# A pre-norm transformer layer with a mixture of experts on one core: routing work and weight loads placed inside the attention's turns, in one program block

## The reference

```python
x = x + attention(layernorm(x))     # 32 query heads, 8 key/value heads of 64, rotary, causal softmax
x = x + experts(layernorm(x))

gate_logits = einsum('bsd,de->bse', x, gate_kernel)          # 8 experts
top_k_weights, top_k_indices = top_k(gate_logits, 2)
top_k_weights = softmax(top_k_weights)
h0 = x @ w0[e]; h1 = x @ w1[e]                                # 256 -> 512
out = sum over the 2 chosen e of weight * (silu(h0) * h1) @ wo[e]   # 512 -> 256
```

## Time and profile before

| | us |
|---|---|
| median of 3 runs | 856.08 (851.24 to 856.58) |
| profiled execution | 854.13 |
| its span, first to last instruction | 852.2 |
| last matmul of attention ends | 556.6 |
| first expert matmul starts | 635.3 |

### The profile page before, as it was taken

How to read it: one execution, slowest core, us unless ns; L and a number is a source line. 1 busy time by engine, 2 the same in 40 slices (tenths; PEclk the granted TensorE clock), 3 DMA queues, 4 the chain that set the end, 5 groups by cost and what they waited for, 6 DMA issues and landing times. The chain is left out here.

```text
span 852.2 us, 18997 instructions
## 1 busy us (share of the span) xinstructions
PE 753.5 (88%) x5895; PEld 637.9 (75%) x5895; DVE 493.2 (58%) x1943; ACT 481.4 (56%) x1537; POOL 460.3 (54%) x690
## 2 busy tenths in 40 slices
PE   3699999999999999999999999826039999999994
PEld 2578888888888888888888888622027888888883
DVE  5797666666666667667567667384942333333331
ACT  1568777777777777777777777625212222222221
POOL 1456656556566565565565666346633545444452
PEclk9899999999999999999999999968559999999998
DMA  5434122122121221221221212058631223333230
GB/s 191 133 112 106 36 60 65 37 63 62 40 64 51 50 63 46 56 60 42 63 54 48 63 40 63 14 169 253 202 137 26 47 45 53 52 54 52 45 50 2
DMA packets 51905, 61.16 MB, mean 72 GB/s; under 512 B 10368, under 2 KB 45440, under 8 KB 51552
## 3 DMA queue, kind: packets, MB, share of 16 engines
q1 hardware_dynamic: 40144, 48.48, 20.0%
q0 software_dynamic: 7488, 9.36, 6.8%
q10 hardware_dynamic: 4176, 2.11, 0.9%
HBM read 26.34 MB, written 9.32 MB: 42 GB/s over the span
## 5 line engine op out<-in xcount | busy, mean ns | idle before, releaser
L818 POOL TENSOR_SCALAR probs<-exps,inv_sums 128x128 f32<-128x128 f32 x256 | 97.0, 379 | 195.7 <-DVE inv_sums L676 135.3
L557 ACT COPY pT<-probsT 128x384 f32<-128x384 f32 x256 | 122.0, 477 | 80.4 <-PE probsT L434 80.4
L434 PE MATMUL probsT<-tables,probs 128*128 128x128 f32 x768 | 129.8, 278 | 5.4 <-ACT pT L557 4.0
L550 ACT ACTIVATE exps<-masked,neg_max 128x256 f32<-128x256 f32 x256 | 127.5, 498 | 0.0
L819 POOL TENSOR_SCALAR probs<-exps,inv_sums 128x256 f32<-128x256 f32 x256 | 124.4, 486 | 0.0
L548 ACT ACTIVATE exps<-masked,neg_max 128x128 f32<-128x128 f32 x256 | 103.2, 403 | 37.0 <-DVE neg_max L670 36.8
L1411 POOL DMA_INDIRECT out<-y,to_token x39 | 61.9, 1587 | 102.4 <-DVE y L1380 78.2
L421 PE MATMUL scores<-kT,qT 64*128 64x128 f32 (+1 forms) x1024 | 103.3, 342 | 5.1 <-DMA qT<-rotated 5.1
L670 DVE CUSTOM_DVE_ANT_0 masked<-scores,tables 128x256 f32<-128x256 f32 x256 | 107.5, 420 | 0.0
L668 DVE CUSTOM_DVE_ANT_0 masked<-scores,tables 128x128 f32<-128x128 f32 x256 | 72.1, 282 | 54.2 <-PE scores L421 32.4
L434 PEld LDWEIGHTS probsT<-tables,probs 128*128 128x128 f32 x768 | 87.2, 141 | 19.5 <-issue 9.7
(11 more groups left out here) (156 smaller groups left out, 1876.4 us busy)
## 6 DMA issues: line engine op xcount, KB each, us to landing
qT<-rotated SPq DMA_DIRECT2D x256, 64.0 KB, 2.2
kT<-k_cos SPq DMA_DIRECT2D x64, 128.0 KB, 3.4
experts_w_out<-w_in SPq DMA_DIRECT2D x16, 512.0 KB, 4.6
raw<-w_attn SPq DMA_DIRECT2D x20, 256.0 KB, 3.3
experts_w_out<-w_out SPq DMA_DIRECT2D x2, 2048.0 KB, 9.7
out<-x_all SPq DMA_DIRECT2D x8, 256.0 KB, 2.3
xn_rows<-experts_w_out ACTq DMA_DIRECT2D x4, 512.0 KB, 4.5
x_all<-x SPq DMA_DIRECT2D x1, 1792.0 KB, 10.6
```

Source lines behind the costliest of these rows:

```text
L434: mm = nc.tensor.transpose(p_bank[:, at:at + P], probs[:, h, at:at + P], ident)
L550: nc.scalar.activation(exps[:, h, P:3 * P], masked[:, h, P:3 * P], ACT.Exp, bias=neg_max[:, h, 1:2], scale=-1.0, accum_out=sums[:, h, 1:2] ...
L557: nc.scalar.copy(pT[:, n % 2, h, :], p_bank[:, 0:3 * P]).then_inc(pT_done, 1)
L818: nc.gpsimd.tensor_scalar(probs[:, h, 0:P], exps[:, h, 0:P], inv_sums[:, h, 0:1], 1.0, ALU.mult, ALU.mult)
```

## The change

The three program blocks become one, and each function returns the lists of its engines, which are called one after the other: attention's, routing's tail, the experts'. SBUF is laid out so that the expert weights of expert e, 16 KB per partition (`experts_w`, slot e: part 0 is hi, part 1 is where the raw half lands and is later overwritten with lo), lie over attention buffers that are free at a known point: slots 0 and 1 over the q weights, 2 over k and v, 3 and 4 over the output weights, 5 over kT, qT and v_all, 6 over pT and oT, 7 over probs, exps and tables. `w_out` of expert e lies over xT, k_cos, by_cos, rotated, xn, masked and the first rows of x_all.

In the turns of batches 1 to 7 the second layer norm of the batch before is computed two tiles at a time, stored to DRAM and taken to logits. PE gets three new steps at a turn's end: "t" (g = 5, four transposes), "l" (g = 7, four matmuls) and, in turn (7, 3), "r", the ranks of the first 12 tiles (batches 0 to 5). The last batch chooses experts for these 12 tiles, makes their lane codes, and loads and splits the first expert slots. POOL no longer subtracts; DVE makes all low parts. Newton takes three steps of three operations. The identity has its own small DMA at the start. After attention, `tail_*` does the rest: the last batch's layer norm, its logits, choice and ranks, rows, codes and tokens, and slots 3, 7, 5, 4 and 6. The first expert matmul waits for all 16 half slots (`slot_split`).

The core of the diff:

```diff
+FIRST_BATCHES = 6
+FIRST_TILES = FIRST_BATCHES * TT
...
     def projects(b, g):
...
+        if g in (5, 7) and b > 0:
+            return {5: "t", 7: "l"}[g], b - 1, 0
+        if (b, g) == (LAST, 3):
+            return "r", 0, 0
...
@@ sync, turn(b, g) @@
+            if g == 5 and b > 0:
+                rt["store_rows"](sp, b - 1)
...
+            if b == LAST:
+                preload(g)
...
+        def preload(g):
+
+            if g == 1:
+                rt["load_w_out"](sp, 7)
+            if g == 2:
+                sp.wait_ge(q_ps, LAST * KV_HEADS + 4)
+                rt["load_slot"](sp, 0, 0)
+            if g == 3:
+                rt["load_slot"](sp, 0, 1)
...
+                rt["load_slot"](sp, 2, 0)
+            if g == 4:
+                rt["load_slot"](sp, 2, 1)
...
+                rt["load_w_out"](sp, 2)
+            if g == 5:
+                sp.wait_ge(q_ps, TURNS)
+                rt["load_slot"](sp, 1, 0)
+                rt["load_slot"](sp, 1, 1)
+                rt["load_w_out"](sp, 0)
+                rt["load_w_out"](sp, 1)
+            if g == 6:
...
+                rt["load_w_out"](sp, 4)
+            if g == 7:
+                sp.wait_ge(s_ps, (TURNS - 1) * GROUP)
+                rt["load_slot"](sp, 3, 0)
+                rt["load_slot"](sp, 3, 1)
...
+        sp.wait_ge(exp_done, TURNS * GROUP)
+        rt["load_w_out"](sp, 5)
+        rt["load_w_out"](sp, 6)
+        sp.wait_ge(pT_ps, TURNS * GROUP)
+        rt["load_slot"](sp, 7, 0)
+        rt["load_slot"](sp, 7, 1)
+        sp.wait_ge(o_ps, TURNS)
+        rt["load_slot"](sp, 5, 0)
+        rt["load_slot"](sp, 5, 1)
+        sp.wait_ge(y_ps, BATCH)
+        for slot in (4, 6):
+            rt["load_slot"](sp, slot, 0)
+            rt["load_slot"](sp, slot, 1)
...
@@ tensor, turn(b, g) @@
-            whole = projects(b, g)[0] is not None
+            whole = projects(b, g)[0] in ("x", "k", "v")
...
@@ scalar, turn(b, g) @@
+                if what == "t":
+                    rt["copy_rows"](act, of)
...
+            if (b, g) == (LAST, 3):
+                rt["gap_exp"](act, 0)
+            if b == LAST and g in (4, 5):
+                rt["slot_hi"](act, {4: 0, 5: 2}[g], 0)
             exponentials(b, g, 2)
+            if b == LAST and g in (4, 5):
+                rt["slot_hi"](act, {4: 0, 5: 2}[g], 1)
+            if (b, g) == (LAST, 6):
+                rt["store_weights"](act, 0)
+            if (b, g) == (LAST, 7):
+                rt["slot_hi"](act, 1, 0)
             exponentials(b, g, 3)
+            if (b, g) == (LAST, 7):
+                rt["slot_hi"](act, 1, 1)
             copy_probs(b, g, 0)
...
@@ vector, turn(b, g) @@
+            if g == 2 and b > 0:
+                rt["row_stats"](dve, b - 1)
             split_in_slot(b, g, 2)
             inverses(b, g, 2)
+            if g == 3 and b > 0:
+                rt["row_moments"](dve, b - 1)
+                rt["row_newton"](dve, 0, 1)
+            if g == 4 and b > 0:
+                rt["row_newton"](dve, 1, 3)
+                rt["row_normalise"](dve, b - 1)
...
+            if b == LAST:
+                routing(g)
...
+        def routing(g):
+
+            if g == 0:
+                rt["choose"](dve, 0, 0)
+            if g == 1:
+                rt["choose"](dve, 0, 1)
+                rt["both"](dve, 0)
+            if g == 5:
+                rt["choice_weights"](dve, 0)
+                rt["first_lanes"](dve)
+            if g == 6:
+                rt["lane_codes"](dve, 0)
+                rt["slot_lo"](dve, 0, 0)
+                rt["slot_lo"](dve, 0, 1)
+            if g == 7:
+                rt["slot_lo"](dve, 2, 0)
+                rt["slot_lo"](dve, 2, 1)
...
         out_lo(LAST, KV_HEADS - 2)
         inverses(LAST, KV_HEADS - 1, 3)
+        rt["read_logits"](dve, LAST - 1)
+        for half in range(2):
+            rt["slot_lo"](dve, 1, half)
         out_lo(LAST, KV_HEADS - 1)
...
+    def tail_tensor(pe):
+        transposes(pe, LAST)
+        gate_logits(pe, LAST)
+        ranks(pe, r["rank_bank"], 1)
         pe.wait_ge(block_lane_done, 1)
...
+    def tail_scalar(act):
+        act.wait_ge(y_added, BATCH)
+        nc.scalar.dma_start(t["out"][LAST].rearrange("(t p) e -> p t e", p=P),
+                            r["x_all"][:, LAST * TT:TILES, :]).then_inc(out_started, 16)
+        for half in range(2):
+            slot_hi(act, 3, half)
+        act.wait_ge(xn_done, BATCH)
+        nc.scalar.dma_start(rows_dram(LAST), xn).then_inc(xn_out, 16)
+        copy_rows(act, LAST)
+        for half in range(2):
+            slot_hi(act, 7, half)
+        gap_exp(act, 1)
+        store_weights(act, 1)
+        for half in range(2):
+            slot_hi(act, 5, half)
         act.wait_ge(block_hot_done, 1)
         nc.scalar.activation(block_codes[:, :, 1, :], block_codes[:, :, 1, :], ACT.Copy,
                              scale=lane).then_inc(block_lane_done, 1)
+        for e in (4, 6):
+            for half in range(2):
+                slot_hi(act, e, half)
...
+    def slot_hi(act, e, half):
+        act.wait_ge(slot_in[e][half], 16)
...
+        nc.scalar.copy(r["ew"][:, e, 0, cols], r["ew"][:, e, 1, cols].bitcast(F32)).then_inc(slot_hi_done[e], 1)
...
+    def slot_lo(dve, e, half):
+        dve.wait_ge(slot_hi_done[e], half + 1)
...
+        nc.vector.tensor_tensor(r["ew"][:, e, 1, cols], r["ew"][:, e, 1, cols].bitcast(F32),
+                                r["ew"][:, e, 0, cols].bitcast(F32), ALU.subtract).then_inc(slot_split, 1)
...
+    def tail_vector(dve):
+        row_stats(dve, LAST)
+        row_moments(dve, LAST)
+        row_newton(dve, 0, 3)
+        row_normalise(dve, LAST)
+        for half in range(2):
+            slot_lo(dve, 3, half)
+        read_logits(dve, LAST)
+        choose(dve, 1, 0)
+        choose(dve, 1, 1)
+        both_hot(dve, 1)
...
+        row_lanes(dve, 1)
+        lane_codes(dve, 1)
+        choice_weights(dve, 1)
...
+        for half in range(2):
+            slot_lo(dve, 7, half)
         dve.wait_ge(pairs_ps, 1)
...
+        for e in (5, 4, 6):
+            for half in range(2):
+                slot_lo(dve, e, half)
...
@@ experts, tensor @@
         pe.wait_ge(xT_lo_done, 1)
         expert = owner(0)
+        pe.wait_ge(r["slot_split"], 2 * EXPERTS)
         hidden(0, expert, 0)
```

More of the change, by code:

```diff
@@ L94, in shape_constants, with attention @@
     groups = np.arange(1, 2 * TILES + 1, dtype=np.float32)
[L95 to L100, removed]
+    route = np.concatenate([np.tile(np.concatenate([rev, steps, starts, lanes, groups, earlier]), (P, 1)),
+                            lanes[:, None]], 1)
+    squares = np.concatenate([before, ones], 1)
+    return [np.ascontiguousarray(a, np.float32) for a in (attn, ident, route, squares)]
+def attention(nc, ctx, sems, t, r, rt):
     def sb(name, shape, dt=F32):
@@ new lines, in ranks @@
+    def ranks(pe, bank, part):
+        tiles = range(TILES)[tiles_of(part)]
+        end = len(tiles) * EXPERTS
+        pe.wait_ge(both_done, part + 1)
+        for i, tile in enumerate(tiles):
+            m = both[:, tile, :].rearrange("p (o e) -> p o e", o=1).to_broadcast([P, len(tiles) - i, EXPERTS])
+            nc.tensor.matmul(bank[:, (i + 1) * EXPERTS:end + EXPERTS].rearrange("p (t e) -> p t e", e=EXPERTS),
+                             ones_16, m, start=(i == 0), stop=False, skip_group_check=True)
+        mm = nc.tensor.matmul(bank[:, 0:end], before_16, both[:, tiles_of(part), :].rearrange("p t e -> p (t e)"),
+                              start=False, stop=True, skip_group_check=True)
+        mm.then_inc(ranks_ps, 1)
@@ new lines, in copy_rows, with gap_exp, store_weights @@
+    def copy_rows(act, b):
+        act.wait_ge(xT_ps, b + 1)
+        if b > 0:
+            act.wait_ge(logits_ps, b)
+        nc.scalar.copy(xT, x_bank[:, :].rearrange("p (k q) -> p k q", k=KT)).then_inc(xT_done, 1)
+    def gap_exp(act, part):
+        act.wait_ge(gap_done, part + 1)
+        tiles = tiles_of(part)
+        nc.scalar.activation(gap[:, tiles], gap[:, tiles], ACT.Exp).then_inc(exp_done, 1)
+    def store_weights(act, part):
+        act.wait_ge(weights_done, part + 1)
+        tiles = tiles_of(part)
+        nc.scalar.dma_start(t["xn"].rearrange("(t p) e -> p t e", p=P)[:, tiles, EMB:ROW],
+                            r["weights"][:, tiles, :]).then_inc(weights_out, 16)
@@ new lines, in program, with _ @@
+            block = ctx.enter_context(nc.Block())
+            @block.sync
+            def _(sp):
+                at["sync"](sp)
+                ex["sync"](sp)
+            @block.tensor
+            def _(pe):
+                at["tensor"](pe)
+                rt["tensor"](pe)
+                ex["tensor"](pe)
+            @block.scalar
+            def _(act):
+                at["scalar"](act)
+                rt["scalar"](act)
+                ex["scalar"](act)
+            @block.vector
```

740 lines of the change are left out of this document (379 added, 361 removed).

## The result

The changed kernel takes 844.4 us (median of 4 runs, 843.3 to 847.0) against 855.6 in the same comparison: ratio 0.988, 95% interval 0.984 to 0.992. So 11 us faster, where I had forecast 26. The profiled execution took 847.0, its span is 845.2. The direction was right and the size was not.

What follows compares the result with a forecast made beforehand. PE was taken to bound attention turns and experts, with a 78.7 us routing hole between. Profiled 854.1, less 41.4 for the hole, plus 17.3 in attention, gave 830.0 us; range 814 to 848.

Steps and rivals of the forecast that it cites:

- The hole: From last attn_out matmul to first expert matmul: 78.7 us falls to 37.3, 41.4 off, bounds 36 and 46.
- rival 4: Experts do not start early since slots 4 and 6 land late; +5, 835 us; chance 0.05.
- PE's steps: Batches 1 to 7, transposes in turn 5 and small matmuls in turn 7: 0.5 each, 7.0 us; ranks 0.9.
- DVE's pieces in batches 1 to 6: Layer-norm row operations near turn ends: some 1.2 to 1.5 us hide, 0.25 a batch shows, 1.5 in all.
- The start: Start of the kernel, DVE's layer norm before attention: shorter by 7 x 0.2 = 1.4 us.
- The last batch: Routing pieces in the last batch's turns: 9.3 us added, besides PE's steps and ranks.
- Turn 6's piece: Last batch, DVE's four lane_codes and two slot_lo after the last reciprocal: 5.7 us, of which 4.7 shows.
- choose and both: Last batch, choosing experts in turns 0 and 1, 1.4 and 2.1 us: 0.5 shows.
- slot_hi and first_lanes: Last batch, turns 4 and 5: two slot_hi on ACT, first_lanes (2.2) on DVE; 1.0 and 1.2 us show.
- Rival 2: Turns become chain-bound in every batch: 0.82 for all 14 steps, DVE's 12 instead of 1.5; 845 us; chance 0.16.
- Rivals 1, 3 and 4: 1: cover holds everywhere, 817 (0.15); 3: no DVE insertion covered, 881 (0.03); 4: slots 4 and 6 late, 835 (0.05).
- the three signs that I named for being wrong: Middle turns 3 to 5 over half a microsecond longer beyond PE's part; PE's clock falling inside attention; slot_split late through loads.

Runs made afterwards that it cites:

- the two spread versions: Changed kernel with row pieces ahead of the last reciprocal and last batch's routing pieces spread, 825.9 us; that plus ACT's tail order and later first weight pieces, 822.9 us.

## Why the prediction was right or wrong

Of its two sums the hole's held (41.4, measured 40.3). The sum of what attention's turns pay did not: 17.3, measured 32.6, in the four steps told below the hole.

**The hole (right).** 40.3 off against 41.4. POOL's subtractions were what stretched DVE, as the earlier trace rows had it: giving six of sixteen back cost 5.9 us, with the same 32-column operation at 2.20 and 0.19. ACT's order (block_codes behind slot_hi(5)) set the pairs as I had it, and the weight loads were never late, so rival 4 did not come. That it is only 1.1 longer than my sum is in part luck, since terms missed both ways. PE's four transposes, the copy and the gate matmuls took 3.7 where I had 1.7, at the lower level (granted clock 0.50), so DVE got the logits at 8.7 instead of 7.3. The first block-code operation takes 2.38 with POOL idle too, where I took 1.4 and put the rest down to POOL; the codes were done at 19.7 instead of 17.5. Shorter terms gave half of this back, among them the pair matmuls, 2.26 for my 2.8.

The Trainium skill (GPSIMD Engine Reference, section Specifications) names the contention for VectorE's instructions with two SBUF inputs; the run with POOL's subtractions agrees, down to the reductions of one input that kept their 0.19. Its page Trainium Architecture — The Big Picture, section What this means for kernel authors, calls the shared port pair an exclusive lock and not a split of bandwidth. That I had read in one direction only: the divisions of 0.37 that took 1.65 and 2.27 agree with it in the other.

**PE's steps (one term mis-sized).** 0.5 a step was right for the transposes (0.44) and wrong for the logits (0.86), since I counted calls and took a transpose's time for each; halving them took 0.44 off. Over six batches 1.8 too little. The ranks were 0.44 instead of 0.9.

The Trainium skill (FP8 and Floating Point Precision, section TensorE Precision Notes) counts four passes for true FP32. The trace shows two records a call, which neither bears out four nor speaks against them; by the page I should at least have doubted that a full-precision product costs what a transpose costs.

**DVE's pieces in batches 1 to 6 (wrong step).** "Some 1.2 to 1.5 us hide": I read that cover from the idle time before two maxima, the first of turn (4, 5), and the first of turn (7, 7), where the batch is nearly over, and asked who waits for pT. The first to wait is PE's next projection, for the bank that rope_k and x_lo read. 0.96 a batch instead of 0.25; moved ahead of the reciprocal the same pieces cost next to nothing (turn 4 takes 8.73 then, 8.71 before the change). The last batch has these pieces too, and my sum had no term for them there. I also took the first line of the earlier trace rows for a turn. It lies across two; turn (4, 5) itself, 332.77 to 340.04, has PE busy for all of its 7.27, DVE for 5.78 and ACT for 5.33, so DVE had 1.5 to spare where that line shows 2.25. The turns that I called (3, 3) and (3, 5) are of batch 4; nothing hangs on that.

**The start (wrong step).** -1.4, measured +1.5. The 1.4 was there at the first scores and went into ACT's wait for the next weight piece, which SP loads behind the second q projection's moves. I had looked at what becomes shorter and not at the next transfer on which the chain hangs.

**The last batch (right mechanism, mis-sized).** 17.0 against 11.2. Turn 6's piece cost 4.3, near the 4.7, plus up to 4 through the clock. The two other misses are sums of serial parts that I took as parallel: choose and both showed 1.2 instead of 0.5, and turns 4 to 6 became 5.0 longer (less PE's 0.44), where I had 2.2 for slot_hi and first_lanes; 1.1 of the 5.0 were the row pieces, gone when these moved, and 3.9 slot_hi and first_lanes. The tail without PE's logits made 9.0 for my 6.6, less than what PE's matmuls lost by the clock (busy 18.8 in the changed kernel, 14.9 without turn 6's piece).

**The rivals.** Rival 2's 845 is nearly the measured time, but not by its reasons: it had 0.82 for every step and 12 for DVE (measured 0.44 and 0.86, and 5.8), and nothing of the start or of the last batch. Rivals 1, 3 and 4 did not occur. Of the three signs that I named for being wrong, PE's clock falling inside attention showed. Turns 3 to 5 lengthened by 0.97 together beyond PE's part, but by 0.48 in each of two, just under the half microsecond that I had set, so that sign was set too coarsely.

## What to carry to other kernels

What the limiting engine gets is paid in full (PE's transposes 0.44, its logits 0.86 a batch). On the other engines work costs by its place more than by its size: the last batch's routing pieces cost some 11 us less when they stood where their engine was waiting anyway (between an exponential and its reciprocal) or behind the last division and copies. Before moving work, follow the queue behind it to every reader of a shared buffer, and add up pieces on two engines when one's result opens the other's. A saving at the start of a pipeline counts only if the next transfer also comes earlier, or nothing urgent stands behind the wait for it.

## What the runs showed of the hardware

- DVE and POOL hold each other up in both directions, by whole instructions: 32-column DVE operations 0.19 or 2.04 to 2.26 beside POOL's 1024-column subtraction; POOL's 128-column division 0.37 or 1.65 to 2.27 beside DVE's.
- PE's waits of 2.2 and 4.4 us in turns 6 and 7 of the changed kernel were each followed by matmuls at the lower level (1.2 GHz), and the same tail then took 24.9 to 28.9 us at a mean granted clock of 0.91 to 0.73 in six profiles, the largest scatter of one stretch in these traces. In the two spread versions, whose longest wait in the last batch was 1.8, it took 19.1 in both, at 1.00.
- From 15.5 to 17.9 us of the changed kernel the profile's clock reads 1.00 while matmuls of 256 columns start 0.21 us apart, the spacing that goes with the lower level elsewhere (0.12 at the upper).
- Plain f32 matmuls with 128 weight columns and 8 moving ones cost 0.22 us a call at a granted clock of 1.00 and are two records.
